# A GRU over 256 steps on one core: a third of the seven block products formed over pairs of groups

## The reference

```python
x = x + conv(x, cond)            # depthwise, causal, K = 16
def cell(h, x):
    gi = x @ W_ih + b_ih         # 512 -> 1536
    gh = h @ W_hh + b_hh
    i_r, i_z, i_n = split(gi, 3); h_r, h_z, h_n = split(gh, 3)
    r = sigmoid(i_r + h_r); z = sigmoid(i_z + h_z)
    n = tanh(i_n + r * h_n)
    return (1 - z) * n + z * h
x = x + scan(cell, cond, x)      # 256 steps, one after another
```

## Time and profile before

| what | value |
|---|---|
| time, median of 3 runs | 984.76 us (984.54 to 985.01) |
| profiled execution | 985.27 us, span 983.5 us |
| TensorE busy | 972.4 us, 99% |
| VectorE busy | 882.0 us, 90% |
| GpSimd busy | 563.8 us, 57% |
| ScalarE busy | 511.6 us, 52% |
| TensorE's granted clock, mean | 1.000 |

### The profile page before, as it was taken

The page is one execution under the profiler, slowest core; times in us unless marked ns, Lnnn a source line. Parts: engine busy times, 40 slices in busy tenths (PEclk is TensorE's granted clock), DMA queues, the critical chain, the costliest instruction groups (busy, mean ns, idle before and its releaser), DMA issues.

```text
span 983.5 us, 63779 instructions
## 1 busy us (share of the span) xinstructions
PE 972.4 (99%) x26644; PEld 800.5 (81%) x26644; DVE 882.0 (90%) x3075; ACT 511.6 (52%) x2154; POOL 563.8 (57%) x1597
## 2 busy tenths in 40 slices
PE   8999999999999999999999999999999999999997
PEld 5898899888888888888888888888888888888875
DVE  7879999999999999999999999999999988887555
ACT  4334455555555555555555555555555555555543
POOL 6556665655555555555555555655556555555442
PEclk9999999999999999999999999999999999999999
DMA  8721001010010101101010010100101000000000
GB/s 306 76 38 36 26 16 33 16 41 20 20 33 16 37 20 31 30 13 37 15 37 25 17 37 12 41 20 20 37 14 36 14 26 25 12 28 5 22 17 13
DMA packets 67600, 32.43 MB, mean 33 GB/s; under 512 B 44528, under 2 KB 65648, under 8 KB 67312
## 3 DMA queue, kind: packets, MB, share of 16 engines
q1 hardware_dynamic: 66880, 28.25, 11.0%
q10 hardware_dynamic: 432, 0.11, 0.0%
HBM read 19.86 MB, written 8.49 MB: 29 GB/s over the span
## 4 chain that ended last, share of the span: by engine, by line
PE 96%; DVE 2%; DMA 0%; issue 0%; POOL 0%; ACT 0%; POOLq 0%; DVEq 0%; SPq 0%
PE pg L810 67%; PE pcv L615 8%; PE pg L605 8%; PE pg L615 4%; PE pcv L625 4%; PE pcv L635 3%; PE pg L595 1%; DVE x L1013 1%; DMA xs<-x 0%; PE pcv L605 0%; PE pcv L825 0%; DVE x L1003 0%; DVE gt L1075 0%; POOL nzh L572 0%; DVE hp L1100 0%
## 5 line engine op out<-in xcount | busy, mean ns | idle before, releaser
L810 PE MATMUL pg<-whh,hp 128*32 128x192 f32 x16384 | 717.1, 326 | 5.9 <-DVE hp L1100 3.5
L810 PEld LDWEIGHTS pg<-whh,hp 128*32 128x32 f32 x16384 | 521.8, 110 | 130.3 <-DVE hp L1100 11.9
L1031 DVE SCALAR_TENSOR_TENSOR pcv<-xb,cnd,pcv 128x256 f32<-128x256 f32 (+2 forms) x588 | 315.0, 536 | 6.9
L983 ACT ACTIVATE rz<-gt 128x64 f32<-128x64 f32 x512 | 136.2, 266 | 304.6 <-DVE gt L1075 277.2
L572 POOL TENSOR_TENSOR nzh<-rz,hp 128x32 f32<-128x32 f32 x512 | 158.1, 309 | 222.1 <-ACT rz L983 220.4
L1075 DVE STREAM_TRANSPOSE gt<-pg 128x128 f32<-128x128 f32 x512 | 161.9, 316 | 50.1 <-PE pg L810 42.9
L988 ACT ACTIVATE nzh<-an 128x32 f32<-128x32 f32 x512 | 120.9, 236 | 126.7 <-DVE an L1087 126.7
L1100 DVE TENSOR_TENSOR_SCAN hp<-zcp,nzh 128x96 f32<-128x96 f32 x512 | 173.1, 338 | 11.9 <-ACT nzh L988 9.4
L1087 DVE TENSOR_TENSOR_SCAN an<-rz,gn 128x64 f32<-128x64 f32 x512 | 149.7, 292 | 26.3 <-ACT rz L983 25.9
L985 ACT ACTIVATE zcp<-gt 128x32 f32<-128x32 f32 x512 | 111.1, 217 | 0.0
L1079 DVE STREAM_TRANSPOSE gn<-pg 128x64 f32<-128x64 f32 x512 | 107.2, 209 | 0.0
(11 more groups left out here) (111 smaller groups left out, 883.1 us busy)
## 6 DMA issues: line engine op xcount, KB each, us to landing
xb<-x SPq DMA_DIRECT2D x96, 94.0 KB, 1.9
out<-x SPq DMA_DIRECT2D x60, 128.0 KB, 1.8
wih<-w_ih SPq DMA_DIRECT2D x4, 768.0 KB, 7.9
whh<-w_hh SPq DMA_DIRECT2D x4, 512.0 KB, 11.9
xw<-x SPq DMA_DIRECT2D x24, 64.0 KB, 3.3
whh<-w_hh SPq DMA_DIRECT2D x4, 256.0 KB, 13.5
xb<-x SPq DMA_DIRECT2D x16, 62.0 KB, 1.8
tz<-taps SPq DMA_DIRECT2D x12, 64.0 KB, 3.6
```

Of the source, the lines that this page charges most:

```text
L810: i = pe.matmul(pg[t // 2 % Q][f][D * j:D * (j + 1), 0:IN], hp[:, t % 2, 2 * c + 1 - t % 2:2 * c + 3 - t % 2, :, 1].rearrange("p u b -> p ...
L983: act.activation(rz[:, f, :, :, 1].rearrange("p g (c b) -> p (g c) b", b=B), gt[:, f, :, u], ACT.Sigmoid).then_inc(s_rz[f], 1)
L1031: dve.scalar_tensor_tensor(x1_of(c, a, b)[:, lo:hi] if lag == K - 1 else sums, xx[:, c, (K - 1 - lag) * B + lo:(K - 1 - lag) * B + hi], cn ...
```

## The change

P5 of two neighbouring groups is formed in the same way as P1 and P7: kind 2, from g = 12 (`DEEP5`) on. Its x side is the sum of two chunks each, formed by the new `halves_added` in two parts (`x5`), its weights are eight more half forms (`DEEP5_FORM`). In return the whole product in `p5` goes, and so does one of GpSimd's sums a group (`mixed` 1). P5's start values (`dl`, `delta_of`) take the place of the fixed `delta` in q12.

The shared sums of kinds 1 and 2 no longer stand in `stage` but in the unused columns END to END + 192 of the gate bank `pg[(2g+1) % 3][1]` (`spare_of`), the front in step r = 2, the back at the head of the group in r = 3. ScalarE seeds and copies them by themselves (`eb`). Kind 0 stays in `stage`. The tables `second` and `fourth` are new, and GpSimd's `between` is written out anew for even and odd groups. The buffers lie in `windows`, which held the convolution's first windows before.

```diff
+DEEP5 = 12
+DEEP5_FORM = [28, 29, 32, 33, 35, 36, 37, 40]
...
+            def halves_added(g, c):
+
+                pool.wait_ge(s_long, convolved(4 * g, 3 + c))
+                if deep5(g - 1):
+                    pool.wait_ge(s_sx, formed(g - 1, 2))
+                eight = x1[:, :, 4 * g % KEEP * B:(4 * g % KEEP + 8) * B].rearrange("p c (q i n) -> p c q i n", q=2, i=2)
+                pool.tensor_tensor(x5[:, :, c, :], eight[:, c, :, 1, :], eight[:, CH + c, :, 1, :], ALU.add).then_inc(s_x5, 1)
...
             def between(t):
...
+                elif r == 3 and g % 2 == 0:
+                    if job1(g):
+                        deep_mixed(1, g + 2, 1)
+                        deep_mixed(1, g + 2, 2)
+                    early_third_sum(g + 1)
+                    if job1(g):
+                        deep_mixed(1, g + 2, 4)
+                    if deep5(g):
+                        seeds(2, g, 3)
+                    if job0(g + 1):
+                        deep_mixed(0, g + 4, 3)
+                elif r == 0:
+                    second_sum(g)
+                    if job0(g):
+                        deep_mixed(0, g + 3, 1)
+                        deep_mixed(0, g + 3, 2)
+                    if job1(g - 1):
+                        seeds(1, g + 1, 1)
+                    if job2(g):
+                        halves_added(g + 1, 0)
...
+                elif r == 3:
+                    if job2(g):
+                        halves_added(g + 1, 1)
+                        deep_mixed(2, g + 1, 1)
+                        deep_mixed(2, g + 1, 2)
+                    early_third_sum(g + 1)
+                    if job0(g):
+                        deep_mixed(0, g + 3, 4)
+                        seeds(0, g + 3, 1)
+                    if job1(g + 1):
+                        differences(g + 3)
...
+            def front12(g):
+
+                if job12(g):
+                    pe.wait_ge(s_seed12, 2 * jobs12(g) - 1)
...
+                    i = front_of_pair(1, g + 2, spare_of(g)) if job1(g) else front_of_pair(2, g + 1, spare_of(g))
+                    i.then_inc(s_front12, 1)
...
             def p5(g):
 
                 pe.wait_ge(s_e27, g - FAST + 1)
+                if deep5(g):
+                    return own_parts(g, 2)
...
                 elif r == 2 and ready(g):
                     p3(g)
                     second_part(g, 2)
                     fourth_part(g, 2)
+                    front12(g)
                 elif r == 3:
+                    back12(g)
...
+                if r == 3 and job12(g):
+                    act.wait_ge(s_front12, jobs12(g))
+                    act.activation(eb[:, 1, :], spare_of(g), ACT.Copy).then_inc(s_e12, 1)
+                    act.wait_ge(s_e12, 2 * jobs12(g) - 1)
+                    act.activation(spare_of(g)[:, HALF:IN], jd[:, 1, :] if job1(g) else jd5[:, :],
+                                   ACT.Copy).then_inc(s_seed12, 1)
```

More of the change, by code:

```diff
@@ L249, in deep, with deep5, job0, job1 @@
             return DEEP <= g <= LAST
+        def deep5(g):
+            return DEEP5 <= g <= LAST
         def job(g):
             return DEEP - 3 <= g <= LAST - 3
[L255 to L261, removed]
+        def job0(g):
+            return job(g) and g % 2 == 1
+        def job1(g):
+            return job(g) and g % 2 == 0
+        def job2(g):
+            return g % 2 == 1 and deep5(g + 1)
+        def job12(g):
+            return job1(g) or job2(g)
+        def jobs12(g):
+            return sum(job12(i) for i in range(g + 1))
+        def nth(kind, g):
+            return (g - (DEEP5 if kind == 2 else DEEP)) // 2 + 1
+        def parts_formed(g):
+            return [2, 4] if deep5(g) else [1, 2, 4] if deep(g) else [3, 1, 2, 4]
         def formed(g, i):
-            before = 4 * (min(g, DEEP) - FAST) + 3 * max(g - DEEP, 0)
-            return before + {3: 1, 1: 2, 2: 3, 4: 4}[i] - (1 if deep(g) else 0)
+            return sum(len(parts_formed(n)) for n in range(FAST, g)) + parts_formed(g).index(i) + 1
         def raw(kind, g, grp, c):
+            if kind == 2:
+                return x5[:, grp, c, :]
             if kind:
@@ L488, in deep_mixed, with seeds @@
+            def seeds(kind, g, i):
+                from_, done = copied(kind), s_d[kind]
                 if i == 1:
                     if kind:
-                        pool.wait_ge(s_s3, (g - DEEP) // 2 + 1)
+                        pool.wait_ge(s_e12, 2 * jobs12(g - 1 if kind == 2 else g - 2))
                     else:
-                        front_chunks_ready(g)
-                    pool.tensor_tensor(into[:, 0], raw(kind, g, 1, 0), raw(kind, g, 1, 1), ALU.add).then_inc(s_sl, 1)
+                        pool.wait_ge(s_e4, g - 3 - FAST + 1)
+                    pool.tensor_copy(seed_part(kind, g, 0), threes(from_[:, 1, 0:HALF])).then_inc(done, 1)
@@ L497, in deep_mixed @@
                 elif i == 3:
[L498 to L515, removed]
+                    pool.wait_ge(done, 3 * (nth(kind, g) - 1) + 2)
@@ new lines, in seeds, with second_sum, early_third_sum, product_sums @@
+                    pool.tensor_tensor(seed_part(kind, g + 1, 1), seed_part(kind, g + 1, 0), threes(from_[:, 0, HALF:IN]),
+                                       ALU.add).then_inc(done, 1)
+            def second_sum(g):
+                if not deep5(g):
+                    mixed(g, 1)
+                mixed(g, 2)
+            def early_third_sum(g):
+                if ready(g) and not deep(g):
+                    mixed(g, 3)
+            def product_sums(g):
+                mixed(g, 4)
+                seven = e7[:, :] if g >= DEEP - 3 else ev[:, 1, IN:]
+                pool.wait_ge(s_e27, g - FAST + 1)
+                if g >= DEEP - 3:
+                    pool.wait_ge(s_e7, g - (DEEP - 3) + 1)
+                pool.tensor_tensor(q21[:, RZ:END], ev[:, 1, 0:IN], seven, ALU.add).then_inc(s_q21, 1)
@@ new lines, in last_sums @@
+            def last_sums(g, between=None):
+                seven, n = e7[:, :] if g >= DEEP - 3 else ev[:, 1, IN:], g - FAST + 1
+                pool.wait_ge(s_e4, n)
+                if deep5(g):
+                    pool.wait_ge(s_d[2], 3 * nth(2, g) - (1 if g % 2 == 0 else 0))
+                pool.tensor_tensor(q12[:, RZ:END], ev[:, 0, 0:IN], delta_of(g) if deep5(g) else delta[:, :],
+                                   ALU.add).then_inc(s_q12, 1)
+                if between:
+                    deep_mixed(*between)
+                pool.wait_ge(s_q12, n)
+                pool.tensor_tensor(q22[:, RZ:END], q12[:, RZ:END], seven, ALU.add).then_inc(s_q22, 1)
@@ L558, in between @@
                     weights(t - FORM[0])
[L559 removed]
+                for n, at in enumerate(DEEP_FORM + DEEP5_FORM):
                     if t == at:
```

262 lines of the change are left out of this document (174 added, 88 removed).

## The result

The changed kernel takes 988.16 us (median of 7 runs, 987.91 to 988.62), the kernel before beside it 984.76 us (984.45 to 985.29). The ratio is 1.0034, 95% interval 1.0025 to 1.0043: slower by 3.4 us. Predicted were 988.6 us, 985.2 to 991.8.

A forecast was written before the change was run, and what follows sets the result against it. TensorE was taken as full (99% busy), with the recurrence as second limit. Terms -2.9 + 0.5 + 0.4 + 5.8 = +3.8 us on the profiled 985.27 gave 989.1, less 0.5 for the median: 988.6 us, range 985.2 to 991.8.

The forecast's parts named there:

- TensorE's price: TensorE, steps 48 to 239: P5 pair costs 3.5 units instead of 4, saving 0.12 us a cycle, -2.9 us in all.
- The floor of 3.62 us: Recurrence through gt, nzh and hp keeps a step at 3.62 us, even with 11 units (0.325 us each, 3.58 us).
- The fourth rival: P5's half products on TensorE cost more than half: +0.11 instead of -0.12 us a cycle, 994 us; chance 0.02.
- Start and end: Steps 24 to 47: new tables and GpSimd's half weights, +0.5 us; steps 242 to 244 above the floor, +0.4 us.
- The window's end: GpSimd waits for the window's last tap, six sums queued before nzh: 0.88 us in six steps, 0.5 in step 235, +5.8.
- The wait is met: Tap result a step sooner or sums short enough at window ends, so the +5.8 falls away: 982.8 us; chance 0.14.
- half the price: GpSimd's burst at window ends costs only 0.4 us each time: +1.4, 986.2 us; chance 0.08.
- Late in every cycle: GpSimd's r=3 burst passes the slack in ordinary steps too, by 0.1 to 0.2 us: 991 to 993.5 us; chance 0.1.
- the room: Ordinary steps r=3 of odd groups: GpSimd's six sums take 1.9 us against 1.70 plus 0.25 slack, leaving 0.05 us.
- TensorE's own wait for L570: Head of the group at window ends: 0.4 us, within time TensorE would stand anyway, so no added cost.
- The sign that did not show: At seven window ends TensorE idles 0.6 to 0.9 us before the next step, released by hp, visible before the recurrence line.

The follow-up runs named there:

- e5: e4, but with P5 whole again for the last two groups (62 and 63) and tables keeping steps from 240 on at 11 units or fewer: 982.12 us.
- e6: The change with P5 never paired (DEEP5 beyond the last group) and P4's halves placed three in step r=3 of odd groups: 985.24 us, ratio 1.0007.
- e1: The change, but in the seven window-end steps GpSimd's second halves_added adds positions two groups earlier, waiting for no tap (P5's values differ): 982.17 us, ratio 0.9977.
- e7: The change with one more GpSimd sum of 128 columns behind the other six, in the seven window-end steps alone: 991.10 us, ratio 1.0067.
- e4: The change with the edits of e2 and e3 together: 982.43 us, ratio 0.9979.
- e8: The change with the same extra sum as e7, but in the other 19 steps r=3 of odd groups: 990.44 us, ratio 1.0061.
- e3: The change, but in the seven window-end steps TensorE does the back of P5's pair at the end of its group, not the head: 987.92 us, ratio 1.0033.
- e2: The change, but in the seven window-end steps GpSimd's three sums needing no new tap stand ahead of the wait: 985.65 us, ratio 1.0012.

## Why the prediction was right, point by point

**TensorE's price.** -0.12 us a cycle forecast, 29.72 to 29.60 measured. The floor of 3.62 us is there, but not in every step of 11 units, as the forecast had it. Behind a full step such a step takes 3.59 us, about TensorE's own time of 3.58 (82 and 87 in the kernel before, 84 and 87 in the change). Only the second of two in a row, 85, takes 3.62. The steps of 11.5 units take about 3.76 us where 3.74 was forecast. The half unit taken away makes one such second step in each cycle where a full one stood, and saves 3.76 - 3.62 = 0.14 us there. The size came out right; that steps of 11 units behind a full one stand at the floor was wrong. The rule of the Trainium skill, "TensorEngine Tiling (Array Packing)", section Instruction Overhead, read as a time beside the columns of each matmul, is not borne out by this trace: sixteen records of 96 columns take 0.33 us (312.77 to 313.10), as against 0.65 for 192. The fourth rival falls.

**Start and end.** +0.5 and +0.4 forecast. Steps 24 to 47 take 1.27 us more (before 117.73 to 208.66, after 117.42 to 209.62), of which 0.85 are step 43's window end (3.78 to 4.63): 0.4. Steps 240 to 247: 28.95 to 29.34, 0.39. e5 shows that these 0.39 are the steps above the floor. Of the 0.4 in steps 24 to 47, 0.2 stand in e6 too, without paired P5. Step 40, where a half weight stands behind six sums, takes 3.94 us instead of 3.77, the +0.15 of the forecast, and in e6, which has the weight but one sum less, 3.75; the rest was not taken apart.

**The window's end.** 0.88 us a step and 0.5 for the last forecast; measured 4.60 against 3.75, 0.85, and for step 235 4.27, 0.52 (the other five take 4.59 to 4.63, step 107 4.72). The pieces: nzh forecast at 2.0 us after gt, measured 1.91; hp scan forecast to end at 2.69, measured 2.67; TensorE's start 2.75, measured 2.72. That the middle fits so well is partly luck. nzh starts 0.09 us sooner than forecast and takes 0.26 us instead of 0.31, but the hp scan starts 0.09 us behind nzh's end instead of 0.06, and takes 0.41 us instead of 0.32; these nearly cancel. e1 and e7 show the cause, one by taking the wait away, the other by a longer burst.

**Rivals.** "The wait is met" and "half the price" are refuted by the steps of 4.60 us and by e1, which gives the whole back. The sum of the second was wrong besides: 0.4 us at seven places is 2.8, and with -2.9 and +0.9 that makes +0.8 and 985.6 us, not 986.2. "Late in every cycle" did not come true, and the room was larger than I gave. I had the six sums at 1.9 us; they take 1.8 in an ordinary step (340.88 to 342.67), so nzh starts at its usual 0.70 us after gt, and by e4 and e8 could come 0.35 us later. I wrote 0.05, having left out the 0.15 us by which hp is early for TensorE and having priced L551 with its wait at 0.47 us, where it takes 0.41. That room is what I mis-sized, and the chance of 0.1 rested on it; the sum did not.

**TensorE's own wait for L570.** "Falls in the time in which it would stand anyway" is right for the change (e3) and hides how near the second lock was: with nzh freed alone, only 0.37 us of the 0.85 come back (e2).

**The sign that did not show.** I wrote that TensorE would be idle for 0.6 to 0.9 us before the next step, in seven gaps released by hp, and that the page would show more idle time before the recurrence line. It does not (3.5 us before, 3.4 us in the change, six waits each). The idle time is there, 0.66 us in step 75, but 0.35 of it stands at the head of the group, for L570, and the other 0.31 the profile does not count. Only in e3 is it one gap of 0.66 us before the recurrence. So the sum had the length of the step right and the place of the wait wrong.

**Numbers.** Sum +3.8, measured +3.4 on the medians and +3.0 on the two spans. The profiled execution of the kernel before was 0.5 us above its median, that of the change 0.1 us, hence the 0.4 us between the two. Of the 0.8 us between the sum and the spans, 0.3 lie in the first 24 steps, of which the sum counts nothing, 0.2 each in the cycles (24 x 0.13) and the window ends, 0.1 in steps 24 to 47. The first part is no effect of the change that can be shown: in its trace and those of e1 to e8, which do the same up to there, step 24 begins anywhere from 117.12 to 117.48.

## What to carry to other kernels

Read what stands in a queue behind each new wait before you count what the change saves: here 3.1 us of matmuls were won, and seven waits of an engine that is busy for 62% of the time cost 5.6. Work that doesn't need the awaited value goes ahead of the wait, and the consumer on the next engine as far back as it can: both had to be moved, since moving the sums alone left TensorE's wait, and moving TensorE's part alone left GpSimd's. When steps have a floor, spread work so that no step stands above it; units saved in a step that is at the floor buy nothing.

## What was not expected of the hardware

The hp scan takes 0.32 us in an ordinary step and 0.41 us in the long ones (313.78). In the latter it begins while GpSimd's addition to the output is running, which reads SBUF too:

```profile
313.65 0.32 POOL L470 TENSOR_TENSOR x<-x,hp 128x64 f32<-128x64 f32 x1
```

The same 0.41 us stands in e4 and e8, where the two overlap as well, and in e4 the scan does not wait before it (311.67, right behind the transpose), so the way it is released is not the cause. In all ten traces together 64 hp scans begin under the addition with 0.19 to 0.20 us of it left, and each ends 0.21 to 0.22 us after the addition does. The scans that begin with less than 0.08 us of it left take 0.31 to 0.36 us, as those do that meet no instruction of GpSimd.

The scan an shows the same. In step 75 it begins at 312.17, 0.13 us before L567 ends, and takes its usual 0.29 us. Where more is left it grows with it, most in step 40 of the change, where the half weight (L503) is formed (the first two lines), and in step 107 (the other two):

```profile
181.13 0.60 POOL L503 TENSOR_TENSOR windows<-wt,windows 128x192 f32<-128x192 f32 x1
181.18 0.69 DVE L1289 TENSOR_TENSOR_SCAN an<-rz,gn 128x64 f32<-128x64 f32 x1 [0.21 <-ACT rz L1185]
...
431.43 0.26 POOL L567 TENSOR_TENSOR windows<-windows 128x32 f32<-128x32 f32 x1
431.46 0.37 DVE L1289 TENSOR_TENSOR_SCAN an<-rz,gn 128x64 f32<-128x64 f32 x1
```

Both end 0.14 to 0.15 us after GpSimd's instruction, and so do all 27 scans an of the ten traces that begin with over 0.155 us left of a sum other than nzh. It works the other way round too. In an ordinary step nzh begins behind the scan an, takes 0.31 us and ends 0.07 us after it; where no scan is running it takes 0.26 us (313.43):

```profile
342.62 0.29 DVE L1289 TENSOR_TENSOR_SCAN an<-rz,gn 128x64 f32<-128x64 f32 x1
342.67 0.31 POOL L713 TENSOR_TENSOR nzh<-rz,hp 128x32 f32<-128x32 f32 x1
```

The Trainium skill, "SBUF — State Buffer", section Who interferes with whom, says that a VectorE instruction with two SBUF inputs contends with a GpSimd one that reads SBUF, and calls it an exclusive lock in which the order of issue decides who is held up. These rows agree: the later one is held until the earlier is over, and it costs nothing as long as the overlap is shorter than some 0.15 us of the scan an. The prediction looked at the scan an alone, which came first and keeps its 0.29 us; the price was on nzh. For the late nzh it means 0.09 us more on the path, because the addition stands between nzh and the hp scan. Whether moving the addition behind the second nzh gives them back was not tried.
